# Sixteen-head attention: the causal mask of a diagonal added by one 128-row product per head instead of two 64-row products

## The chip, the cores and the metric

The kernel is one program on one core of a Trainium2 chip. The metric is the time on the device in microseconds, the median of several runs. The core has a matrix engine (PE; its weight loads are shown as PEld), a vector engine (DVE), a scalar engine (ACT), a general engine (POOL) and a queue that issues transfers (SP, shown as SPq).

## The reference

Four transformer layers run on 16 batches of 512 positions, each position a vector of 128. Each layer modulates, normalises, applies an attention, then a feed-forward part. The attentions of layers 0 and 1 are the ones that matter here: 16 heads of 8 dimensions each, causal.

```python
# layer 0; layer 1 is alike, without rope and biases, and its mask adds -1e10
scores = jnp.einsum('bhqd,bhkd->bhqk', Q, K)
causal = jnp.triu(jnp.ones((n, n), dtype=bool), k=1)
scores = jnp.where(causal, -jnp.inf, scores)
attn = jax.nn.softmax(scores / jnp.sqrt(jnp.float32(HEAD_DIM)), axis=-1)
ctx = jnp.einsum('bhqk,bhkd->bhqd', attn, V)
```

Layer 3 also has 16 heads, but no mask. Layer 2 has one wide head. Layer 1's feed-forward part is itself a small transformer with a local attention; it adds its band mask in its own way (lines 2334 to 2342: a product of 128 rows with the identity, then the scores in 64 rows) and is not changed, but its rows are used below.

## The kernel before, in words

`heads16_phase` (line 375) does the 16-head attention of layers 0, 1 and 3. It works through **steps**, one batch apart, and each step has 20 **slots** in a causal layer. The work of three batches overlaps in a step: the maxima of batch i, the probabilities of batch i-1 (or i-2), the projections of batch i+2.

In each slot PE does, in this order: a projection or other full product where the slot has one (`project`, line 614; output product, line 693; V, line 702; transposes of the maxima, line 687); then `a_pair`, the scores of a slot with queries on the partitions, into two PSUM banks of `PA`; then `b_pair`, the scores with keys on the partitions, into two banks of `PB`; then, in 16 of the 20 slots, `pv_pack` (line 674), probabilities times values for four heads, in tiles of 128 rows by 32 columns.

Heads go in pairs. Q and K are split into bf16 terms, so that a head's product has 48 rows (51 in `b_pair`, with the maximum). Head e of a pair lies on partitions 64e and up. So the two products of a pair use the two 64-row halves of the array, and PE runs them side by side. Because of the causal shape a score product is 128, 256, 384 or 512 columns wide, and a slot holds one or two such segments of a head, each with one 128 x 128 diagonal block. `Stream` (line 343) lays the segments out. In every five slots, `a_pair` has 8 diagonals per head (1, 2, 2, 1, 2) and `b_pair` has 8 (1, 1, 2, 2, 2).

On the diagonal block half the scores must be masked. `mask` (inner function, lines 616 to 627) adds -1e30 there by further products into the same bank. It splits the 128 mask rows into two halves of 64 rows: `net.select[rows, 0]` and `net.select[rows, 1]` are the upper and lower 64 rows of the identity, as weights of 64 rows by 128 columns, and `net.select[rows, 2]` or `[rows, 3]` holds the mask's triangle. The half that reaches all columns takes 128 columns per diagonal, the other 64. Each is done for e = 0 and e = 1, on the two halves of the array. All products of `a_pair` and `b_pair` are thus in tiles of 64 rows.

DVE reads `PA` with one maximum-reduction per slot (line 938) over both banks; `PA` has two such pairs of banks, so PE may be two slots ahead. ACT reads `PB` with one exponential per head (line 784), and `PB` has three single banks: `b_pair` of a slot may start once the first exponential of the slot before is done. PE, DVE and ACT each take their work strictly in the order of the code and wait by semaphores (`pa_made`, `pa_used`, `pb_made`, `pb_used`). In slot 14 DVE also waits for a transfer (the sums, line 930), and in four slots (two in layer 1) DVE first takes a projection out of `PA` (line 908 or 910).

`modulation_phase` (line 88) opens the program. SP issues the loads one after another: modulation input and weights, constants, eight small loads for `select` (lines 120 to 123), then `X` in four loads. ACT's first operation (line 131) waits for all loads but `X`, and starts a chain ACT, DVE, PE (line 168), DVE that ends the phase.

Of the kernel before, what the change touches and what calls it, by code (L numbers as in the profile page):

```python
# [7 lines left out]
BF16 = mybir.dt.bfloat16  # L8
# [6 lines left out]
P = 128  # L15
# [51 lines left out]
def load_shared(net, ctx):  # L67
    nc, d = net.nc, net.d

    def sb(name, shape, dt=F32):  # L70
        return ctx.enter_context(nc.sbuf_tensor(name, shape, dt))

    net.passed = nc.alloc_semaphore("passed")
    net.X = sb("X", [P, B, S])
    net.MOD = sb("MOD", [P, 4, 6, B])
    net.ident = sb("ident", [P, P])
    net.center = sb("center", [P, P])
    net.mean = sb("mean", [P, P])
    net.ident_b = sb("ident_b", [P, P], BF16)
    net.H = sb("H", [P, B, S])  # L80
    net.eps = sb("eps", [P, 1])
    net.w3 = sb("w3", [P, B * 3])
    net.chosen = sb("chosen", [1, B * 2], U32)
    net.mask_qk = sb("mask_qk", [P, P], BF16)
    net.select = sb("select", [P, 4, P], BF16)


def modulation_phase(net):

    nc, d = net.nc, net.d  # L90
    with ExitStack() as ctx:
        def sb(name, shape, dt=F32):
            return ctx.enter_context(nc.sbuf_tensor(name, shape, dt))

        cT = sb("cT", [P, 4, B])
        sig = sb("sig", [P, 4, B])
        wm = sb("wm", [P, 4, 6 * P])
        maskf = sb("maskf", [P, 5, P])
        ge = sb("ge", [P, 4, B])
        ab = sb("ab", [P, 4, B])  # L100
        ps = ctx.enter_context(nc.psum_tensor("mod_ps", [P, 4, 6, B], F32))
        loaded = nc.alloc_semaphore("mod_loaded")
        x_loaded = nc.alloc_semaphore("x_loaded")
        ex = nc.alloc_semaphore("mod_exp")
        si = nc.alloc_semaphore("mod_silu")
        mm = nc.alloc_semaphore("mod_products")
        ch = nc.alloc_semaphore("mod_dve_chain")
        block = ctx.enter_context(nc.Block())

        @block.sync  # L110
        def _(sp):
            sp.dma_start(cT[:], d["cT"].rearrange("l p b -> p l b")).then_inc(loaded, 16)
            sp.dma_start(wm[:], d["wmod"].rearrange("l p n -> p l n")).then_inc(loaded, 16)
            sp.dma_start(net.ident[:], d["k_ident"]).then_inc(loaded, 16)
            sp.dma_start(net.center[:], d["k_center"]).then_inc(loaded, 16)
            sp.dma_start(net.mean[:], d["k_mean"]).then_inc(loaded, 16)
            sp.dma_start(maskf[:, 4], d["k_mask"][0]).then_inc(loaded, 16)
            for e in range(2):
                rows = slice(64 * e, 64 * e + 64)
                sp.dma_start(maskf[rows, 0], d["k_ident"][0:64]).then_inc(loaded, 16)  # L120
                sp.dma_start(maskf[rows, 1], d["k_ident"][64:128]).then_inc(loaded, 16)
                sp.dma_start(maskf[rows, 2], d["k_mask"][0, 0:64]).then_inc(loaded, 16)
                sp.dma_start(maskf[rows, 3], d["k_mask"][1, 64:128]).then_inc(loaded, 16)
            for b in range(0, B, 4):
                sp.dma_start(net.X[:, b:b + 4], d["xT"][:, b:b + 4]).then_inc(x_loaded, 16)
            sp.wait_ge(x_loaded, 64)

        @block.scalar
        def _(act):
            act.wait_ge(loaded, 96 + 128)  # L130
            nc.scalar.activation(sig[:], cT[:], ACT.Exp, scale=-1.0).then_inc(ex, 1)

        @block.vector
        def _(dve):
            n = [0]

            def link(ins):
                n[0] += 1
                ins.then_inc(ch, 1)
                dve.wait_ge(ch, n[0])  # L140

            dve.wait_ge(ex, 1)
            link(nc.vector.tensor_scalar(sig[:], sig[:], 1.0, None, ALU.add))
            link(nc.vector.reciprocal(sig[:], sig[:]))
            nc.vector.tensor_tensor(sig[:], sig[:], cT[:], ALU.mult).then_inc(si, 1)
            nc.vector.memset(net.eps[:], 1e-5)
            nc.vector.tensor_copy(net.ident_b[:], net.ident[:])
            nc.vector.tensor_copy(net.mask_qk[:], maskf[:, 4])
            nc.vector.tensor_copy(net.select[:], maskf[:, 0:4])
            dve.wait_ge(mm, 1)  # L150
            M = net.MOD
            link(nc.vector.tensor_copy(M[:], ps[:]))
            for j in (1, 4):
                link(nc.vector.tensor_scalar(M[:, :, j], M[:, :, j], 1.0, None, ALU.add))
            for j in (2, 5):

                link(nc.vector.tensor_scalar(ge[:], M[:, :, j], 0.0, None, ALU.is_ge))
                link(nc.vector.tensor_scalar(ge[:], ge[:], 2.0, -1.0, ALU.mult, ALU.add))
                link(nc.vector.tensor_tensor(ab[:], M[:, :, j], ge[:], ALU.mult))
                link(nc.vector.tensor_scalar(ab[:], ab[:], 0.25, None, ALU.max))  # L160
                link(nc.vector.tensor_tensor(M[:, :, j], ge[:], ab[:], ALU.mult))

        @block.tensor
        def _(pe):
            pe.wait_ge(si, 1)
            for l in range(4):
                for j in range(6):
                    last = nc.tensor.matmul(ps[:, l, j], wm[:, l, j * P:(j + 1) * P], sig[:, l],
                                            start=True, stop=True)
            last.then_inc(mm, 1)  # L170
# [204 lines left out]
def heads16_phase(net, name, layer, causal, rope, w_sum):  # L375

    nc, X, H, d = net.nc, net.X, net.H, net.d
    gate = net.MOD[:, layer, 2]
    scale = float(1.0 / np.sqrt(np.float32(DH8)))
    with ExitStack() as ctx:  # L380
        def sb(n, shape, dt=F32):
            return ctx.enter_context(nc.sbuf_tensor(name + n, shape, dt))
# [19 lines left out]
        st = Stream(causal, rope)  # L402
# [12 lines left out]
        PA = ctx.enter_context(nc.psum_tensor(name + "PA", [P, 4, S], F32))  # L415
        PB = ctx.enter_context(nc.psum_tensor(name + "PB", [P, 3, S], F32))
# [43 lines left out]
        loaded = nc.alloc_semaphore(name + "loaded")  # L460
# [129 lines left out]
        def _(pe):  # L590
# [22 lines left out]
                at_least(pe, pa_used, used_a.before(i, ("Q", n)))  # L613
                nc.tensor.matmul(PA[:, 2 * made_a.slot(par, ("Q", n))], wqk[:, n], H[:, i + 2], start=True, stop=True).then_inc(pa_made, 1)

            def mask(bank, diagonals, pieces):

                k0 = diagonals[0] // P
                by = (diagonals[-1] - diagonals[0]) // P or 1
                done = []  # L620
                for which, of, c0, c1, to in pieces:
                    for e in range(2):
                        rows = slice(64 * e, 64 * e + 64)
                        out = bank(e).rearrange("p (k c) -> p k c", c=P)[:, k0:diagonals[-1] // P + 1:by, to:to + c1 - c0]
                        piece = net.select[rows, of, c0:c1].unsqueeze(1).broadcast_to([64, len(diagonals), c1 - c0])
                        done.append(nc.tensor.matmul(out, net.select[rows, which], piece, start=False, stop=which == pieces[-1][0]))  # L626
                return done[-2:]

            def a_pair(b, i, par, k):
                bank = 2 * made_a.slot(par, ("a", k))  # L630
                at_least(pe, pa_used, used_a.before(i, ("a", k)))
                if k % st.per_group == 0:
                    stacked[k // st.per_group].wait(pe, b, 64)
                done = []
                for n, (pr, t, c) in enumerate(st.a[k]):
                    w = P * (t + 1) if causal else S
                    for e in range(2):
                        rows = slice(64 * e, 64 * e + TERMS)
                        done.append(nc.tensor.matmul(PA[:, bank + e, c:c + w], QS[rows, par, pr, t * P:(t + 1) * P], KS[rows, par, pr, 0:w],  # L639
                                                     start=(n == 0), stop=not causal))  # L640
                if causal:
                    done = mask(lambda e: PA[:, bank + e], [c + P * t for pr, t, c in st.a[k]], [(0, 2, 0, 128, 0), (1, 2, 0, 64, 64)])
                for mm in done[-2:]:
                    mm.then_inc(pa_made, 1)

            def b_pair(b, i, par, k, s):
                bank = [ring_b.slot(0, ("b", s, e)) for e in range(2)]
# [3 lines left out]
                done = []  # L651
                for n, (pr, t, c) in enumerate(st.b[k]):
                    q0 = P * t if causal else 0
                    for e in range(2):
                        rows = slice(64 * e, 64 * e + TERMS + 3)
                        done.append(nc.tensor.matmul(PB[:, bank[e], c:c + S - q0], KS[rows, par, pr, t * P:(t + 1) * P], QS[rows, par, pr, q0:S],  # L656
                                                     start=(n == 0), stop=not causal))
                if causal:
                    done = mask(lambda e: PB[:, bank[e]], [c for pr, t, c in st.b[k]], [(0, 3, 64, 128, 0), (1, 3, 0, 128, 0)])
                for mm in done[-2:]:  # L660
                    mm.then_inc(pb_made, 1)

# [2227 lines left out]
```

## Time and profile before

| what | us |
|---|---|
| median of 3 runs | 6144.11 (6137.29 to 6147.71) |
| the profiled execution | 6168.16 |
| its span, first to last instruction | 6166.0 |
| PE busy, of the span | 5082.9 (82%) |
| DVE busy | 3501.2 (57%) |
| ACT busy | 3147.4 (51%) |
| POOL busy | 2512.3 (41%) |

The mean granted PE clock is 0.899 of full speed. The stages follow each other with little overlap, so a stage's time is read from its own window: layer 0's causal stage has its masks from 100.2 to about 719 us of the span, layer 1's up to 1800.6 us. A PE record's length includes some 0.16 us of latency after its last column, which overlaps the next product; what a product keeps the array for is therefore read from the distance between the starts of two records. A line with "x2" or "x4" on PE joins records that follow each other closely.

### The profile page before, as it was taken

The page shows a single profiled execution, that of the slowest core. Times are in us where ns is not written, and L with a number is a line of the kernel's source. Part 1 is how long each engine was busy: PE and PEld are TensorE (multiplying, and loading weights), DVE is VectorE, ACT ScalarE, POOL GpSimd, SP SyncE. Part 2 cuts the span into 40 slices and gives each one's busy share as a digit, 9 for nine tenths or more (in the row PEclk, how much of TensorE's full clock was granted, in tenths as well). Part 3 has the DMA queues.
Part 4 walks back from the last instruction along what each step waited for, and adds up shares of the span by engine and source line. Part 5 has one row for each costly group of instructions (what it writes and reads, how often), then busy time and mean ns, then how long its engine had stood idle before and what let it go on. Part 6 is the DMA issues. An engine that isn't in the chain of part 4 may idle for free. (4 is left out here: it accounts for less than half of the span.)

```text
span 6166.0 us, 105844 instructions
## 1 busy us (share of the span) xinstructions
PE 5082.9 (82%) x38207; PEld 2620.5 (42%) x38217; DVE 3501.2 (57%) x5633; ACT 3147.4 (51%) x7104; POOL 2512.3 (41%) x2126
## 2 busy tenths in 40 slices
PE   6999779888876999988999998874237999874995
PEld 2444334344433666643566663342112222241784
DVE  5777422487744666643666654565338999730233
ACT  2666633366663666642566663342014888831542
POOL 3333100222206888841788871116562232116025
PEclk7999989899997999998999999986557999976997
DMA  3343111133310000011000000011112333211123
GB/s 99 108 120 110 40 45 48 57 111 103 108 44 20 6 7 8 5 56 45 6 8 6 6 3 4 2 28 41 36 32 65 95 89 96 59 46 49 52 76 90
DMA packets 329515, 312.95 MB, mean 51 GB/s; under 512 B 78758, under 2 KB 279106, under 8 KB 327106
## 3 DMA queue, kind: packets, MB, share of 16 engines
q1 hardware_dynamic: 312642, 285.77, 16.2%
q0 software_dynamic: 16384, 20.69, 1.2%
q8 instruction: 303, 4.96, 0.3%
q14 instruction: 186, 1.52, 0.1%
HBM read 172.15 MB, written 136.32 MB: 50 GB/s over the span
## 5 line engine op out<-in xcount | busy, mean ns | idle before, releaser
L784 ACT ACTIVATE a_prob<-a_PB 128x512 f32<-128x512 f32 x2304 | 1253.4, 598 | 456.9 <-PE a_PB L626 342.7
L674 PE MATMUL a_PO<-a_prob,a_V 128*32 128x256 f32 (+3 forms) x8192 | 715.0, 422 | 22.6 <-ACT a_cn L757 22.3
L938 DVE TENSOR_REDUCE a_blocks<-a_PA 128x8 f32<-128x1024 f32 x512 | 602.0, 1214 | 37.4 <-PE a_PA L626 35.0
L941 DVE TENSOR_REDUCE a_neg<-a_PA 128x2 f32<-128x1024 f32 x512 | 590.8, 1212 | 34.8 <-PE a_PA L639 34.7
L639 PE MATMUL a_PA<-a_KS,a_QS 48*128 48x512 bf16 (+3 forms) x3072 | 469.0, 344 | 112.9 <-DVE a_blocks L938 71.0
L2538 DVE TENSOR_REDUCE f1a_neg<-f1a_PA 128x2 f32<-128x384 f32 (+1 forms) x512 | 266.7, 521 | 488.4 <-PE f1a_PA L2340 487.9
L2468 POOL TENSOR_TENSOR f1a_prob<-f1a_prob,f1a_inv 128x384 f32<-128x384 f32 (+1 forms) x512 | 394.2, 773 | 283.3 <-DVE f1a_inv L2542 283.3
L656 PE MATMUL a_PB<-a_QS,a_KS 51*128 51x512 bf16 (+3 forms) x3072 | 448.3, 329 | 56.6 <-ACT a_prob L784 54.9
L2432 ACT ACTIVATE f1a_pt<-f1a_PT 128x512 f32<-128x512 f32 (+1 forms) x512 | 278.7, 544 | 348.5 <-PE f1a_PT L2349 344.7
L2425 ACT ACTIVATE f1a_prob<-f1a_PA,f1a_neg 128x192 f32<-128x192 f32 (+1 forms) x1024 | 405.3, 404 | 67.9 <-DVE f1a_neg L2538 67.8
L639 PEld LDWEIGHTS a_PA<-a_KS,a_QS 48*128 48x128 bf16 x3072 | 123.5, 94 | 635.5 <-DVE a_blocks L938 199.6
L2477 POOL TENSOR_TENSOR f1a_ss<-f1a_ss,f1a_power 128x16 f32<-128x16 f32 x128 | 372.5, 2910 | 0.9
L838 POOL TENSOR_TENSOR a_qk<-a_qk,a_t 128x512 f32<-128x512 f32 x64 | 81.3, 1270 | 688.2 <-DVE a_t L908 688.2
L2473 POOL TENSOR_TENSOR f1a_qk<-f1a_qk,f1a_rot 128x1024 f32<-128x1024 f32 x128 | 301.0, 2352 | 65.0 <-DVE f1a_rot L2524 65.0
L2349 PE MATMUL f1a_PT<-ident,f1a_prob 128*128 128x128 f32 x1792 | 308.0, 289 | 1.9 <-POOL f1a_prob L2468 1.1
L2360 PE MATMUL f1a_PO<-f1a_pt,f1a_v 128*64 128x128 f32 x3584 | 308.8, 287 | 0.1
L2340 PE MATMUL f1a_PA<-f1a_kT,f1a_qT 64*128 64x192 f32 (+1 forms) x2048 | 293.0, 363 | 0.0
L2030 POOL DMA_INDIRECT f_rows<-tokens_out,f_slot x128 | 132.5, 1035 | 314.0 <-DMA tokens_out<-f_rows 220.2
L674 PEld LDWEIGHTS a_PO<-a_prob,a_V 128*32 128x32 f32 x8192 | 163.3, 108 | 227.6 <-issue 126.8
L2481 POOL TENSOR_TENSOR f1a_qk<-f1a_qk,f1a_ss 128x1024 f32<-128x1024 f32 x128 | 243.5, 1903 | 10.1
L2413 ACT ACTIVATE f1a_sq<-f1a_PJ 128x1024 f32<-128x1024 f32 x128 | 131.2, 1025 | 216.8 <-PE f1a_PJ L2321 216.8
L1180 ACT ACTIVATE f_hid<-f_ph,f_bias 128x512 f32<-128x512 f32 x192 | 131.8, 687 | 199.5 <-PE f_ph L1148 199.0
(416 smaller groups left out, 10391.4 us busy)
## 6 DMA issues: line engine op xcount, KB each, us to landing
a_spill<-a_qkp SPq DMA_DIRECT2D x96, 384.0 KB
a_QS<-a_spill SPq DMA_DIRECT2D x384, 96.0 KB, 2.5
a_KS<-a_spill SPq DMA_DIRECT2D x384, 96.0 KB, 2.5
a_spill<-a_qkp SPq DMA_DIRECT2D x96, 256.0 KB
a_raw<-a_cn SPq DMA_DIRECT2D x192, 72.0 KB
a_spill<-a_qkp SPq DMA_DIRECT2D x96, 128.0 KB
f_rows<-tokens_in SPq DMA_DIRECT2D x78, 128.0 KB
tokens_out<-f_rows SPq DMA_DIRECT2D x78, 128.0 KB
```

Of the source, the lines that this page charges most:

```text
L639: done.append(nc.tensor.matmul(PA[:, bank + e, c:c + w], QS[rows, par, pr, t * P:(t + 1) * P], KS[rows, par, pr, 0:w], start=(n == 0), sto ...
L656: done.append(nc.tensor.matmul(PB[:, bank[e], c:c + S - q0], KS[rows, par, pr, t * P:(t + 1) * P], QS[rows, par, pr, q0:S], start=(n == 0) ...
L674: mm = nc.tensor.matmul(PO[32 * j:32 * j + 32, first:last], V[:, par, t, 8 * e + pr], prob[:, k % st.ring, e, c + first - q0:c + last - q0 ...
L784: nc.scalar.activation(prob[:, k % st.ring, e], PB[:, ring_b.slot(0, ("b", s, e))], ACT.Exp, scale=scale).then_inc(pb_used, 1)
L938: nc.vector.tensor_reduce(to, of, AX, ALU.max).then_inc(pa_used, 1)
L941: nc.vector.tensor_reduce(neg[:, t, pr], PA[:, bank:bank + 2], AX, ALU.max, negate=True).then_inc(pa_used, 1)
L2349: tr = nc.tensor.transpose(PT[:, 2 * e + kt], prob[:, u % 4, e, kt * P:(kt + 1) * P], ident)
L2360: mm = nc.tensor.matmul(PO[e * DH64:(e + 1) * DH64, hp], v[:, par, t - 1 + kt, h * DH64:(h + 1) * DH64], pt[:, u % 2, e, kt], start=(kt == ...
L2425: nc.scalar.activation(prob[:, u % 4, e, c0:], PA[:, u % 2, e, c0:2 * P], ACT.Exp, bias=neg[:, u % 4, e:e + 1], accum_out=total[:, u % 4, ...
L2468: nc.gpsimd.tensor_tensor(pr, pr, inv[:, u % 4].unsqueeze(2).broadcast_to([P, 2, 2 * P - c0]), ALU.mult).then_inc(normed.sem, 1)
L2473: nc.gpsimd.tensor_tensor(qk[:, t], qk[:, t], rot[:], ALU.add).then_inc(joined.sem, 1)
L2477: nc.gpsimd.tensor_tensor(ss[:, t], ss[:, t], power[:], ALU.pow).then_inc(rooted.sem, 1)
```

## The change

`mask` becomes one product per head over all 128 rows: the identity `net.ident_b` (bf16, 128 x 128, already there) as weights, and the whole mask block as the moving operand, 128 columns per diagonal. It is done first for e = 0, then for e = 1. The order of everything else stays. `net.select` goes, a second mask tile `net.mask_kq` comes, and seven of the small loads of the opening go.

```diff
-    net.select = sb("select", [P, 4, P], BF16)
+    net.mask_kq = sb("mask_kq", [P, P], BF16)
...
-            for e in range(2):
-                rows = slice(64 * e, 64 * e + 64)
-                sp.dma_start(maskf[rows, 0], d["k_ident"][0:64]).then_inc(loaded, 16)
-                sp.dma_start(maskf[rows, 1], d["k_ident"][64:128]).then_inc(loaded, 16)
-                sp.dma_start(maskf[rows, 2], d["k_mask"][0, 0:64]).then_inc(loaded, 16)
-                sp.dma_start(maskf[rows, 3], d["k_mask"][1, 64:128]).then_inc(loaded, 16)
+            sp.dma_start(maskf[:, 0], d["k_mask"][1]).then_inc(loaded, 16)
...
-            act.wait_ge(loaded, 96 + 128)
+            act.wait_ge(loaded, 96 + 16)
...
-            nc.vector.tensor_copy(net.select[:], maskf[:, 0:4])
+            nc.vector.tensor_copy(net.mask_kq[:], maskf[:, 0])
...
-            def mask(bank, diagonals, pieces):
+            def mask(bank, diagonals, of):
...
-                done = []
-                for which, of, c0, c1, to in pieces:
-                    for e in range(2):
-                        rows = slice(64 * e, 64 * e + 64)
-                        out = bank(e).rearrange("p (k c) -> p k c", c=P)[:, k0:diagonals[-1] // P + 1:by, to:to + c1 - c0]
-                        piece = net.select[rows, of, c0:c1].unsqueeze(1).broadcast_to([64, len(diagonals), c1 - c0])
-                        done.append(nc.tensor.matmul(out, net.select[rows, which], piece, start=False, stop=which == pieces[-1][0]))
-                return done[-2:]
+                piece = of[:].unsqueeze(1).broadcast_to([P, len(diagonals), P])
+                return [nc.tensor.matmul(bank(e).rearrange("p (k c) -> p k c", c=P)[:, k0:diagonals[-1] // P + 1:by], net.ident_b[:], piece,
+                                         start=False, stop=True) for e in range(2)]
...
-                    done = mask(lambda e: PA[:, bank + e], [c + P * t for pr, t, c in st.a[k]], [(0, 2, 0, 128, 0), (1, 2, 0, 64, 64)])
+                    done = mask(lambda e: PA[:, bank + e], [c + P * t for pr, t, c in st.a[k]], net.mask_qk)
...
-                    done = mask(lambda e: PB[:, bank[e]], [c for pr, t, c in st.b[k]], [(0, 3, 64, 128, 0), (1, 3, 0, 128, 0)])
+                    done = mask(lambda e: PB[:, bank[e]], [c for pr, t, c in st.b[k]], net.mask_kq)
```

## Rows read from the trace of the kernel before

**Rows 1.** Windows: length, busy us of PE, PEld, DVE, ACT, POOL, PEclk, DMA, GB/s

```profile
101.00:168.70 67.70, 53.96 (x508) 23.63 (x508) 55.94 (x66) 19.04 (x34) 21.24 (x23) 0.74 0.22 72
168.70:612.80 444.10, 413.85 (x5254) 186.18 (x5251) 352.00 (x421) 294.37 (x552) 148.71 (x156) 1.00 0.40 113
612.80:678.10 65.30, 57.95 (x824) 27.37 (x820) 50.11 (x54) 46.39 (x88) 3.81 (x4) 1.00 0.27 67
678.10:722.50 44.40, 34.41 (x412) 12.32 (x408) 5.01 (x14) 33.98 (x65) 3.54 (x4) 0.96 0.10 22
...
1272.70:1698.40 425.70, 382.89 (x5188) 177.28 (x5187) 333.76 (x396) 294.04 (x552) 106.09 (x120) 0.98 0.38 107
1698.40:1763.10 64.70, 57.36 (x812) 26.94 (x814) 50.49 (x53) 46.25 (x87) 3.10 (x3) 0.97 0.27 69
```

**Rows 2.** Groups, 168.7 to 612.8 us: busy us, mean ns | idle before

```profile
L784 ACT ACTIVATE a_prob<-a_PB 128x512 f32<-128x512 f32 x480 | 261.3, 599 | 143.8 <-PE a_PB L626 142.1 <-PE a_PO L674 1.7
L938 DVE TENSOR_REDUCE a_blocks<-a_PA 128x8 f32<-128x1024 f32 x193 | 227.3, 1213 | 8.1 <-PE a_PA L626 8.0
...
L639 PE MATMUL a_PA<-a_KS,a_QS 48*128 48x512 bf16 (+3 forms) x768 | 93.9, 302 | 17.7 <-DVE a_blocks L938 15.6 <-DVE a_halves L938 0.6
L656 PE MATMUL a_PB<-a_QS,a_KS 51*128 51x512 bf16 (+3 forms) x768 | 92.4, 298 | 12.2 <-ACT a_prob L784 11.3
...
L938 DVE TENSOR_REDUCE a_halves<-a_PA 128x8 f32<-128x1024 f32 x48 | 58.5, 1218 | 11.4 <-PE a_PA L626 11.4
```

**Rows 3.** Groups, 1272.7 to 1698.4 us, PE's longest wait

```profile
L639 PE MATMUL a_PA<-a_KS,a_QS 48*128 48x512 bf16 (+3 forms) x768 | 94.7, 305 | 30.9 <-DVE a_blocks L938 30.8
```

**Rows 4.** Line 626: ns min/median/max, first to last start us, shapes

```profile
L626 PE MATMUL a_PA<-select x2560: 187/218/418, 100.6 to 1762.8; 64*128 64x128 bf16 x98, 64*128 64x256 bf16 x60, 64*128 64x64 bf16 x39
```

**Rows 5.** PE timeline, one slot of layer 0: start us, length us

```profile
402.71 0.39 PE L639 MATMUL a_PA<-a_KS,a_QS 48*128 48x512 bf16 x2
402.94 0.25 PE L626 MATMUL a_PA<-select 64*128 64x128 bf16 x4
403.03 0.38 PE L656 MATMUL a_PB<-a_QS,a_KS 51*128 51x512 bf16 x2
403.25 0.25 PE L626 MATMUL a_PB<-select 64*128 64x64 bf16 x4
403.43 0.42 PE L674 MATMUL a_PO<-a_prob,a_V 128*32 128x128 f32 x8
403.78 1.12 PE L614 MATMUL a_PA<-H,a_wqk 128*128 128x512 f32 x2
404.84 0.34 PE L639 MATMUL a_PA<-a_KS,a_QS 48*128 48x384 bf16 x2
```

**Rows 6.** PE timeline, local attention of layer 1

```profile
2502.68 1.02 PE L2321 MATMUL f1a_PJ<-f1a_w,f1a_hs 128*128 128x512 f32 x2
2503.54 0.33 PE L2337 MATMUL f1a_PA<-f1a_band,ident_b 128*128 128x192 bf16 x2
2503.80 0.59 PE L2340 MATMUL f1a_PA<-f1a_kT,f1a_qT 64*128 64x192 f32 x4
2504.32 0.66 PE L2349 MATMUL f1a_PT<-ident,f1a_prob 128*128 128x128 f32 x4
2504.91 0.33 PE L2360 MATMUL f1a_PO<-f1a_pt,f1a_v 128*64 128x128 f32 x2
```

**Rows 7.** Timeline and one transfer (us to landing) of the opening

```profile
3.34 0.44 SPq L117 DMA_DIRECT2D maskf<-in_k_mask  x1
3.82 0.56 SPq L120 DMA_DIRECT2D maskf<-in_k_ident  x1
...
8.90 2.26 SPq L125 DMA_DIRECT2D X<-in_xT  x4
11.20 0.26 ACT L131 ACTIVATE sig<-cT 128x64 f32<-128x64 f32 x1 [9.19 <-DMA maskf<-in_k_mask]
...
wm<-in_wmod SPq DMA_DIRECT2D x1, 1536.0 KB, 6.6
```

## The prediction

> **What bounds the kernel now.** I first cut the two causal stages into windows. From 168.7 to 612.8 us layer 0 does 12 full steps: 241 of the 20-slot steps' maximum reductions lie in it [rows 2], so a step takes 444.1 / 12 = 37.0 us. Layer 1's 12 full steps take 425.7 / 12 = 35.5 us [rows 1]. In layer 0 PE is busy 413.85 of 444.1 us, DVE 352, ACT 294; in layer 1 PE 383 of 426, DVE 334, ACT 294. PE's clock is 1.00 and 0.98, so nearly always at 2.4 GHz. Next I looked at who waits. ACT's exponentials sat idle 143.8 us, nearly all for the mask products of `b_pair`; DVE's reductions 19.5 us for those of `a_pair`; PE's score products only 17.7 + 12.2 us, for DVE and ACT [rows 2], and 30.9 us for DVE in layer 1 [rows 3]. So PE sets the pace, with some waits left, more of them in layer 1.
>
> Last, the timeline, since busy time hides what a product holds the array for. From the score product to the mask are 0.23 us for 512 columns (213 ns at 2.4 GHz), from there to the next scores 0.09 us for 128 + 64 columns (80 ns): both heads of a pair together, nothing lost between scores and masks. From the masks of `b_pair` to the pack at line 674 are 0.18 us for 80 ns of columns [rows 5]. The difference, **0.10 us, appears wherever the shape of the tiles changes** (64x128, 128x32, full 128x128). The local attention shows it in the order that the change makes: line 2321 to 2337, both full 128x128, 0.86 us for 0.85 us of columns (f32 takes four passes, 2048 columns in 0.85); line 2337 to 2340, full to 64 rows, 0.26 us for 2 x 192 columns = 0.16: 0.10 lost; line 2340 to 2349, 64 rows to full, 0.52 us for 0.32: 0.10 lost, and another 0.10 because the first f32 weights after a change are loaded in the open [rows 6]. For bf16 that second part is about 0.01: 0.23 us after a change against 0.22 without one, for the same 512 columns [rows 5]. A change of tile shape with bf16 behind it therefore costs 0.105 us.
>
> **The changes, part by part.**
>
> *The columns.* A 64-row mask pair takes 128 + 64 columns per diagonal with both heads at once; the 128-row products take 128 per diagonal and head, one after the other: 64 more per diagonal. With 16 diagonals per five slots, 64 in a step: 4096 columns, **+1.7 us a step**.
>
> *The tile changes.* Before, a slot is 64-row from the first score to the last mask. After, scores, mask, scores, mask alternate: three more changes in each of 20 slots, and one more after the last mask in the 4 slots without a pack, where the next scores follow directly. From mask to pack there was a change already. 64 changes x 0.105 = **+6.7 us a step**.
>
> *Fewer instructions.* 80 products and their loads fewer a step. Concurrent tiles start 3 to 7 ns apart in line with the slot of [rows 5], about 4 ns for each of 5254 / 12 = 438 records [rows 1]: -0.3 us a step. Loading the same identity twice hides behind the product before it, as the two of line 2337 do (2 x 192 columns and one change fill their 0.26 us [rows 6]).
>
> *Sum for PE.* Layer 0 before: 66048 columns-passes a step (scores 20480, masks 12288, packs 20480, projections 8192, output, V and transposes 4608) = 27.5 us; 39 changes x 0.105 = 4.1; 438 starts x 4 ns = 1.7: own work 33.3 us, so 3.7 of the 37.0 are waits. Layer 1 (59904 columns, 36 changes): 30.5 us, 5.0 of waits. After: 33.3 + 8.1 = **41.4** and **38.6 us**. That is beyond DVE's 352 / 12 = 29 us and ACT's 25 to 28, so most waits vanish: where PE waited for a reduction or an exponential, it now arrives later. What stays? Each step has one wait of DVE for the sums, and projection slots are uneven. I leave 0.6 us a step in layer 0 and 0.9 in layer 1, between none and all of today's 3.7 and 5.0; nearer to none, since PE now leads DVE by 12 and 10 us a step. Steps of 42.0 and 39.5 us: 12 x 5.0 + 12 x 4.0 = **+108 us**.
>
> *The ends of the stages.* The next window, 65.3 and 64.7 us for 39 slots, has no projections but all masks [rows 1]: own work after is 41.4 less the 3.4 us and 4 changes of four projections, 37.5 us a step (layer 1, two projections: 36.7), with 0.6 and 0.9 of waits 39/20 of it is 74 and 73: +17 together. In the first two steps (67.7 us, DVE busy 56 [rows 1]) PE has room: I take +1.5 each, bounds 0 and +10. In the tail (44.4 us, ACT busy 34 [rows 1]) only `b_pair` is left, 20 slots and a few: PE gains 4.6 us of work, much beside ACT; I take +2.5 each, bounds 0 and 4.6. Together **+25**.
>
> *The opening.* Seven loads fewer, 0.64 us of SP each: the `X` loads start at 4.4 instead of 8.90 us. ACT's first operation waited 9.19 us until 11.20 for the last small load. But `wm`, 1.5 MB, issued at 1.23, lands 6.6 us later at 7.8 [rows 7], with four 64 KB constants and the new one behind it. I take 9.7: **-1.5 us**, bounds 0 and -3.4. `X` lands early enough. DVE's copy for `select` lies beside PE's modulation products and costs nothing.
>
> *Not shown by the trace:* a change from 64 rows to full with bf16 on both sides. The nearest rows bound it: 0.08 us (the raw 0.10 less rounding of two starts) below, and above 0.165 us, the whole latency of a product (218 ns for 128 columns of 53 [rows 4]), should it be waited out. I take 0.105, as both neighbours give it. Below it 64 x 0.025 = 1.6 us a step less, above it 3.8 more.
>
> The Trainium skill, TensorE: Matmul & The Clock Gate, section Single matmul latency, has the drain of one product at some 175 ns whatever the clock. Taken as the price of each change that would be 11.2 us a step in place of 6.7; the trace has 0.10 at every change in both layers, so the sum goes by that. The Trainium skill, TensorEngine Tiling, Instruction Overhead, gives each product a floor of some 60 cycles, so that halving the products would save 80 x 25 ns = 2 us a step. Here the 64-column piece does not stand above its columns: 0.09 us hold 192 of them.
>
> Against the profiled 6168.2 us: +108 +25 -1.5 = **+132**. The median lies 24 us below that execution: 6144.1 + 132 = **6276 us**.
>
> **Rivals.**
> 1. *The waits stay* (15%). The time to a finished pair grows too: scores, change, mask e = 0, mask e = 1. If DVE and ACT were released late by as much, today's waits would stay on top. Then all of PE's new work counts: per stage some 1010 changes x 0.105 + 27.3 us of columns - 1.3 = 132; two stages 264, less 1.5: 6406 us. For it: ACT idles 143.8 us for exactly these masks. Against: PE may run two slots ahead of DVE.
> 2. *A change costs the full latency*, 0.165 us (9%). Steps of 45.8 and 43.3 us, 12 x (8.8 + 7.8) = 199, ends +40: 6382 us. Against: six places with 0.10.
> 3. *The changes are hidden* (6%, the other side). If from scores to a mask and back PE loses nothing because the identity stands ready in its second set of weights and products of the same bank follow on, only the 1.7 us of columns stay, and 3.7 and 5.0 us of waits take them in; the opening gains 1.5: 6142.6 us. It decides below (3.7 - 1.7) / 64 = 31 ns a change. Against: line 2337 to 2340 writes one bank and still loses 0.10.
> 4. *The diff does not do what it says*: the products for e = 0 and e = 1 could still run side by side. They can't: both fill all 128 rows. I give it nothing.
>
> **How the numbers follow.** Forecast 70%, on its own from 6220 (no waits left: 12 x (4.4 + 3.1) + ends 15 - 1.5 = +104, and -28 for 28 steps with 64 changes of 0.09 us) to 6350 (2 to 3 us of today's waits stay in each step). To leave out no more than 2 in 10 the range goes on to 6382, the second rival: 6222 to 6385. 0.2% of this kernel, 12 us, is about what a measurement can tell. Faster 0.02 and same 0.04 share the third rival, slower 0.94.
>
> **What would show it.** In the profile after: 2560 mask products at the new line, 128*128; 0.10 us lost on either side of each mask in the timeline; steps of 42.0 and 39.5 us in windows from reduction to reduction; ACT idle for PE well above 143.8 us; PE's idle before lines 639 and 656 under 15 us; ACT's first operation near 9.7 us. I am wrong if the steps come out below 39 us (changes hidden), or above 44 (latency paid or waits kept); if the clock of these windows falls from 1.00 the columns are dearer, which none of these sums has in it.

## The result: 2.1% slower, and where the time went

The changed kernel takes 6274.63 us (median of 4 runs, 6270.95 to 6283.94), against 6144.74 before (4 runs): **ratio 1.0211, interval 1.0198 to 1.0223, +130 us**. Forecast were 6276 us and +132. On a second chip, where the kernel before takes 5972.55 us, it takes 6100.76: ratio 1.0213 (1.0198 to 1.0229), +128 us.

The profiled execution after has a span of 6268.8 us, before 6166.0. Cut at the start of each stage, these +102.8 us are: opening -1.8, causal stage of layer 0 +67.2 (713.4 to 780.6), causal stage of layer 1 +55.4 (669.7 to 725.1), together +120.8; and -18 in stages that no edit touches, 13 of it in the last feed-forward stage (691.2 to 677.8). The profiled execution before lay 24 us over its median, and in the run with the new opening alone (below), where that stage is the same too, it took 675.7: so this is scatter between executions and not the change. So the change costs about 121 us by the traces and 130 by the medians. How far one trace can be trusted shows in that same run: its causal stages differ from the kernel before in nothing, and took 703.4 and 675.6 us in place of 713.4 and 669.7, with steps of 36.8 and 35.6 us in place of 37.0 and 35.5. A difference between two traces of under 10 us in a stage, or under 0.3 us in a step, says little.

The windows of the stages, cut from reduction to reduction as in [rows 1], after (same columns):

```profile
97.20:166.20 69.00, 59.99 (x390) 19.16 (x390) 56.54 (x67) 19.04 (x34) 21.29 (x23) 0.79 0.23 76
166.20:668.80 502.60, 502.60 (x4298) 167.82 (x4294) 356.10 (x420) 298.12 (x553) 149.26 (x156) 1.00 0.35 99
668.80:742.50 73.70, 72.65 (x672) 24.54 (x670) 51.34 (x53) 47.18 (x88) 5.10 (x5) 1.00 0.23 59
742.50:788.00 45.50, 37.13 (x357) 11.15 (x356) 5.05 (x13) 33.97 (x65) 2.27 (x2) 1.00 0.10 21
1338.70:1805.80 467.10, 465.54 (x4228) 157.36 (x4224) 340.58 (x396) 298.08 (x553) 106.80 (x120) 1.00 0.35 99
1805.80:1877.60 71.80, 70.38 (x668) 23.99 (x666) 51.76 (x54) 47.27 (x88) 3.10 (x3) 1.00 0.22 53
```

In the 12 full steps of layer 0 PE is now busy 502.60 of 502.60 us: no gap is left that is longer than the latency in its records. A step takes 41.9 us (502.6 / 12) in place of 37.0; in layer 1 38.9 in place of 35.5. DVE's busy time is 1 to 2% above that before, and spreads over the longer time. The groups of layer 0's window, after, to be laid beside [rows 2]:

```profile
L774 ACT ACTIVATE a_prob<-a_PB 128x512 f32<-128x512 f32 x481 | 261.1, 594 | 197.0 <-PE a_PB L616 197.0
L928 DVE TENSOR_REDUCE a_blocks<-a_PA 128x8 f32<-128x1024 f32 x192 | 231.5, 1219 | 36.4 <-PE a_PA L616 34.6
...
L646 PE MATMUL a_PB<-a_QS,a_KS 51*128 51x128 bf16 (+3 forms) x772 | 94.3, 302 | 0.0
L629 PE MATMUL a_PA<-a_KS,a_QS 48*128 48x512 bf16 (+3 forms) x768 | 93.9, 302 | 0.0
L616 PE MATMUL a_PB<-mask_kq,ident_b 128*128 128x256 bf16 (+1 forms) x480 | 83.8, 256 | 0.0
L616 PE MATMUL a_PA<-mask_qk,ident_b 128*128 128x256 bf16 (+1 forms) x480 | 83.8, 256 | 0.0
L928 DVE TENSOR_REDUCE a_halves<-a_PA 128x8 f32<-128x1024 f32 x48 | 58.7, 1222 | 28.3 <-PE a_PA L616 28.1
```

PE's score products had idled 17.7 and 12.2 us for DVE and ACT [rows 2]; now 0.0 and 0.0 (in layer 1, line 629 idles 1.6). What moved is the waiting: ACT idles 197.0 us for the masks in place of 142.1, DVE's reductions 62.7 in place of 19.4. The mask products are 480 on each side instead of 960, each 256 ns long in the mean instead of 227, as their pieces are wider.

Where PE's new time lies shows in its timeline, after, in one slot of layer 0:

```profile
502.69 0.39 PE L629 MATMUL a_PA<-a_KS,a_QS 48*128 48x256 bf16 x4
503.02 0.39 PE L616 MATMUL a_PA<-mask_qk,ident_b 128*128 128x256 bf16 x2
503.34 0.39 PE L646 MATMUL a_PB<-a_QS,a_KS 51*128 51x512 bf16 x2
503.67 0.28 PE L616 MATMUL a_PB<-mask_kq,ident_b 128*128 128x128 bf16 x2
503.88 0.85 PE L664 MATMUL a_PO<-a_prob,a_V 128*32 128x384 f32 x8
504.66 1.12 PE L683 MATMUL a_PA<-a_heads,a_wo 128*128 128x512 f32 x2
505.72 0.39 PE L629 MATMUL a_PA<-a_KS,a_QS 48*128 48x512 bf16 x2
```

From the scores at 502.69 (2 x 256 columns, 213 ns) to the masks at 503.02 are 0.33 us; from the masks (two products of 256 columns, 213 ns) to the next scores at 503.34, 0.32; from these scores (512 columns) to their masks, 0.33. Each is 0.11 to 0.12 above its columns. Before, the first and the third of these distances were 0.23 and 0.22 with the same columns, and the one between masks and scores 0.09 [rows 5]. From masks to pack (256 columns, 107 ns) are 0.21: the change that was there before and stays.

### The profile page after: what moved, and what is told of

It reads as the page before. It is cut to its first block and busy times, and to the rows that moved or that the text cites. A ratio compares the mean times of both kernels' runs of the same rounds, so it can differ in the third digit from the quotient of the medians.

```text
span 6268.8 us, 100727 instructions
## 1 busy us (share of the span) xinstructions
PE 5298.4 (85%) x35657; PEld 2564.4 (41%) x35657; DVE 3517.5 (56%) x5633; ACT 3158.4 (50%) x7104; POOL 2515.4 (40%) x2126
## 3 DMA queue, kind: packets, MB, share of 16 engines
q0 software_dynamic: 16384, 20.69, 1.2%
## 5 line engine op out<-in xcount | busy, mean ns | idle before, releaser
L928 DVE TENSOR_REDUCE a_blocks<-a_PA 128x8 f32<-128x1024 f32 x512 | 616.6, 1218 | 113.7 <-PE a_PA L616 107.5
L1170 ACT ACTIVATE f_hid<-f_ph,f_bias 128x512 f32<-128x512 f32 x192 | 131.8, 687 | 197.5 <-PE f_ph L1138 197.0
```

The lines of the kernel that those rows point to most:

```text
L928: nc.vector.tensor_reduce(to, of, AX, ALU.max).then_inc(pa_used, 1)
```

## The experiments

The first question was whether the time comes from the changes of tile shape or from the columns (and heads no longer side by side). Two runs change one of them, starting from the kernel before.

**Columns only.** Both 64-row pieces of the mask are made 128 columns wide. `net.select` gets two more blocks (4 and 5) for this, with four more small loads in the opening, which the cut below leaves out.

```diff
-                    done = mask(lambda e: PA[:, bank + e], [c + P * t for pr, t, c in st.a[k]], [(0, 2, 0, 128, 0), (1, 2, 0, 64, 64)])
+                    done = mask(lambda e: PA[:, bank + e], [c + P * t for pr, t, c in st.a[k]], [(0, 2, 0, 128, 0), (1, 4, 0, 128, 0)])
...
-                    done = mask(lambda e: PB[:, bank[e]], [c for pr, t, c in st.b[k]], [(0, 3, 64, 128, 0), (1, 3, 0, 128, 0)])
+                    done = mask(lambda e: PB[:, bank[e]], [c for pr, t, c in st.b[k]], [(0, 5, 0, 128, 0), (1, 3, 0, 128, 0)])
```

> The kernel before with both 64-row pieces of the mask 128 columns wide: the 4096 columns a step that the change adds, with no change of tile shape, and 4 more small loads in the opening (about +2.5 us). Theory: PE's own work grows by 1.7 us a step, to 35.0 and 32.2 us, and today's waits of 3.7 and 5.0 us take in about half: +0.9 us a step, total near 6172 us (6147 to 6200). Rival (the columns are what costs): +100 us or more, near 6250 us.

Measured: ratio 1.0030 (1.0019 to 1.0042), +19 us. Steps of 37.5 and 35.8 us: of 1.7 us more work a step only 0.5 and 0.3 arrive, less than the half that I had set. (All experiments but the last four were timed on two chips on both of which the kernel before takes 5972 us; ratios and differences are against that. The kernel before was profiled on a slower chip only, and steps are compared with that trace; that this is allowed shows below, in the changed kernel's second run.) Its window of layer 0:

```profile
166.50:616.80 450.30, 431.17 (x5254) 192.31 (x5254) 350.75 (x420) 294.26 (x552) 148.57 (x156) 1.00 0.40 111
```

PE is busy 19 us of the window less than its length; in [rows 1] it was 30. Added columns fill gaps first.

**Changes of shape only.** The 64-row masks stay. A product of 128 rows with one zero column is set between scores and mask of each pair.

```diff
                 if causal:
+                    nc.tensor.matmul(PA[:, bank, 0:1], net.ident_b[:], net.mask_qk[:, 0:1], start=False, stop=False)
...
                 if causal:
+                    nc.tensor.matmul(PB[:, bank[0], 0:1], net.ident_b[:], net.mask_qk[:, 0:1], start=False, stop=False)
```

> The kernel before, with one product of 128 rows and a single zero column between the scores and the mask of each a_pair and b_pair: 80 changes of tile shape a step more and hardly any column. Theory: own work 33.3 + 80 x 0.105 + 40 x 0.025 = 42.7 us a step in layer 0 and 39.9 us in layer 1, waits under 0.5 us: steps of 43 and 40 us, total near 6300 us. Rival (changes of shape are hidden, the time comes from columns and lost concurrency): 40 products of one column are 1 us a step, total near 6160 us.

Measured: ratio 1.0308 (1.0291 to 1.0326), +183 us; steps of 43.1 and 40.1 us, as worked out. The total is 27 us above my sum: the two stages are 178 us longer than in the trace before, 129 of it in the 24 full steps and 49 at their ends, where I had counted too little. The timeline of PE in this run:

```profile
502.12 0.38 PE L657 MATMUL a_PB<-a_QS,a_KS 51*128 51x384 bf16 x4
502.43 0.18 PE L660 MATMUL a_PB<-mask_qk,ident_b 128*128 128x1 bf16 x1
502.54 0.34 PE L626 MATMUL a_PB<-select 64*128 64x128 bf16 x4
...
503.38 0.39 PE L639 MATMUL a_PA<-a_KS,a_QS 48*128 48x512 bf16 x2
503.70 0.18 PE L642 MATMUL a_PA<-mask_qk,ident_b 128*128 128x1 bf16 x1
503.81 0.26 PE L626 MATMUL a_PA<-select 64*128 64x128 bf16 x4
503.91 0.33 PE L657 MATMUL a_PB<-a_QS,a_KS 51*128 51x384 bf16 x2
```

From the scores at 503.38 (512 columns) to the one-column product are 0.32 us, 0.11 above the columns; from it to the mask in 64 rows another 0.11, with one column in it. So 80 changes with no columns to speak of cost more than the whole change under study. The rival, that took columns and lost concurrency for the cause, had +15 us here.

**Half of them.** The one-column product in `b_pair` alone.

```diff
                 if causal:
+                    nc.tensor.matmul(PB[:, bank[0], 0:1], net.ident_b[:], net.mask_qk[:, 0:1], start=False, stop=False)
```

> The kernel before with the one-column product of 128 rows in b_pair alone: 40 changes of tile shape a step more, half of the run with both. Theory (PE's own work, and waits that give way): own work 33.3 + 4.2 + 0.5 = 38.0 us in layer 0, 35.2 in layer 1, and 1.5 to 2 us of waits: steps of 39.7 and 37.1 us, +75 us. Rival (each change adds its full price whatever the waits): half of what the run with both added, +91 us.

Measured: ratio 1.0147 (1.0132 to 1.0163), +87 us; steps of 40.0 and 37.3 us, against 39.7 and 37.1 by the theory. The total is nearer to the rival's +91 than to my +75, and layer 0 sides with the rival too: the first 40 changes add 3.0 us a step there and the second 40 add 3.1, so the waits did not take in the first of them and pass on the later ones. Only layer 1 goes as the theory said: 1.8 us for the first 40, 2.8 for the second.

**The changed kernel with fewer changes of shape.** The order in a slot becomes scores, scores, masks, masks: `a_pair` and `b_pair` end before their masks and hand back a function that issues them.

```diff
-                    if has(i):
-                        a_pair(i, i, par, s)
+                    last = []
+                    if has(i):
+                        last.append(a_pair(i, i, par, s))
...
+                    for finish in last:
+                        finish()
```

> The changed kernel with the order inside a slot turned to scores of a, scores of b, mask of a, mask of b: the same products and columns, but 40 changes of tile shape fewer a step (63 instead of 103 in layer 0). Theory (the changes of shape cost): PE's own work falls by 40 x 0.107 = 4.3 us a step, from 41.97 to 37.7 us in layer 0 and from 38.8 to 34.5 us in layer 1; some waits come back (about 1.5 us a step, since a mask of a now also stands behind the wait of b's scores for ACT): steps of 39.2 and 36.3 us, total near 6200 us. Rival (128-row products are dear because the two heads no longer run side by side, and by their number): nothing changes, 6275 us.

Measured: ratio 1.0138 (1.0121 to 1.0155), +81 us: **a third of the loss is won back** with the same products and columns, against +128 for the changed kernel on a chip of the same speed. Steps of 39.9 and 37.0 us, 0.7 above what I expected of each. Its timeline, and two of its waits (us in total, times, longest) in the 12 steps of layer 0:

```profile
502.38 0.39 PE L629 MATMUL a_PA<-a_KS,a_QS 48*128 48x384 bf16 x4
502.61 0.38 PE L649 MATMUL a_PB<-a_QS,a_KS 51*128 51x384 bf16 x4
502.93 0.39 PE L616 MATMUL a_PA<-mask_qk,ident_b 128*128 128x256 bf16 x2
503.15 0.38 PE L616 MATMUL a_PB<-mask_kq,ident_b 128*128 128x256 bf16 x2
503.47 0.64 PE L670 MATMUL a_PO<-a_prob,a_V 128*32 128x256 f32 x8
```

```profile
ACT a_prob L785 <- PE a_PB L616: 174.7, 204, 2.0
...
PEld a_PB L649 <- ACT a_prob L785: 33.0, 68, 0.6
```

Only 502.61 to 502.93 (512 columns) and 503.15 to 503.47 hold a change now; 502.38 to 502.61 and 502.93 to 503.15 are bare columns. The 0.7 us more than expected probably sit in the second view: weight loads for the scores of `b_pair` wait 33.0 us for ACT, in place of 20.7 before the change and 13.2 in the changed kernel, and a mask of `a_pair` now stands behind this wait. No run separates this from other waits.

**A product inside one shape.** The changed kernel with each mask product issued twice.

```diff
-                                         start=False, stop=True) for e in range(2)]
+                                         start=False, stop=again == 1) for again in range(2) for e in range(2)]
```

> The changed kernel with each mask product issued twice (it adds -2e30): 16384 columns and 80 products a step more, no change of tile shape more. Theory: PE is the bound without slack, so the step grows by the columns, 6.8 us, and 80 x 3 ns: steps of 49.0 and 45.9 us, total near 6490 us. Rival (a 128-row product costs its full latency, 0.165 us beyond its columns, wherever it stands): 13 us a step on top of the columns, about 6900 us.

Measured: ratio 1.0564 (1.0546 to 1.0582), +333 us against +345 expected by difference; steps of 48.7 and 45.6 us, +6.8 and +6.7. 16384 columns take 6.8 us: that is the columns and nothing else. With PE busy from end to end, its work enters the time in full:

```profile
170.60:754.60 584.00, 584.00 (x5255) 245.64 (x5256) 359.75 (x421) 298.27 (x553) 149.24 (x156) 1.00 0.30 85
```

Behind another of its shape, a 128-row product costs its columns; what costs extra is the way into and out of its shape.

**Is it PE that sets the pace before?** The kernel before, without mask products.

```diff
-                if causal:
+                if False:
                     done = mask(lambda e: PA[:, bank + e], [c + P * t for pr, t, c in st.a[k]], [(0, 2, 0, 128, 0), (1, 2, 0, 64, 64)])
```

and the same in `b_pair`; the last score product of a bank then closes it.

> The kernel before without any mask product (the mask is left out of layers 0 and 1): PE's own work falls by 12288 columns and 160 products, to 27.6 us a step in layer 0 and 24.7 us in layer 1. Theory: DVE (29 us a step with 12 us of other causes to wait) and ACT now set the pace, so that only part is won: steps of 34 and 33 us, total 70 us below before. Rival (PE alone sets the pace even before): steps of 31.9 and 30.4 us, 150 us below.

Measured: ratio 0.9970 (0.9961 to 0.9979), only -17 us, where I expected -70 and the rival -150. 5.8 us less work of PE a step shorten it by 0.7 us in layer 0 (36.3) and 1.2 in layer 1 (34.3). In its window PE is busy 374.50 of 435.40 us, and its clock is no longer full, 0.95 in place of 1.00:

```profile
164.70:600.10 435.40, 374.50 (x3338) 113.88 (x3334) 348.05 (x420) 294.12 (x553) 148.73 (x156) 0.95 0.41 114
```

```profile
L640 PE MATMUL a_PA<-a_KS,a_QS 48*128 48x512 bf16 (+3 forms) x768 | 98.3, 316 | 43.8 <-DVE a_blocks L940 38.4 <-DVE a_t L910 4.5 <-DVE a_halves L940 0.9
L658 PE MATMUL a_PB<-a_QS,a_KS 51*128 51x512 bf16 (+3 forms) x768 | 97.4, 312 | 16.1 <-ACT a_prob L786 14.7
```

PE's scores wait 43.8 and 16.1 us. One rival has to be looked at: that PE does set the pace and the lower clock ate the gain. A mean of 0.95 is about a tenth of the time at 1.2 GHz instead of 2.4, so the clock can hide at most some 0.05 x 36.3 = 1.8 us a step (an estimate). With it the gain would be 2.5 us in layer 0 and under 3 in layer 1, not 5.8. So PE alone does not set the pace. What else does is read from the waits and not tested: DVE's wait for the transfer of the sums, in the 12 steps of layer 0, is 35.1 us here, 25.1 before and 12.6 in the changed kernel. It grows as PE's work shrinks.

Read together, the runs give roughly one curve. PE's own work is a model, worked out as in the prediction at full clock and with 0.105 us a change; the steps are measured; the last column is their difference:

| kernel | own work, us a step, layer 0 / 1 | step, us | left as waits |
|---|---|---|---|
| no masks | 27.5 / 24.7 | 36.3 / 34.3 | 8.8 / 9.6 |
| before | 33.3 / 30.5 | 37.0 / 35.5 | 3.7 / 5.0 |
| columns only | 35.0 / 32.2 | 37.5 / 35.8 | 2.5 / 3.6 |
| masks last | 37.1 / 34.3 | 39.9 / 37.0 | 2.8 / 2.7 |
| changes in `b_pair` | 38.0 / 35.2 | 40.0 / 37.3 | 2.0 / 2.1 |
| changed kernel | 41.4 / 38.6 | 41.9 / 38.9 | 0.5 / 0.3 |
| changes only | 42.7 / 39.9 | 43.1 / 40.1 | 0.4 / 0.2 |
| masks twice | 48.5 / 45.7 | 48.7 / 45.6 | 0.2 / 0 |

Below some 33 us of PE work a step hardly notices; from 33 to 41 it pays about half in the mean; above 41 it pays nearly all. The curve is not exact: with the masks last there is less work than with the changes in `b_pair`, yet more waiting, so the order in a slot counts too. The change crosses this bend: of its 8.1 us in each step 3.2 to 4.7 were taken in.

**The changed kernel again**, on the second chip.

> The changed kernel once more, beside the runs of this chip, on which the kernel before takes 5972 us in place of 6145. Theory: the difference lies in the two causal stages, which are bound by PE and DVE and not by memory, so it is the same +130 us (6101 us) with steps of 41.9 and 38.9 us. Rival (the difference scales with whatever makes this chip faster): less than 100 us.

Measured: +128 us and steps of 41.9 and 38.9 us, the same to 0.01 us. What makes that chip 173 us faster lies outside these stages: 142 us in the last feed-forward stage (677.8 to 536.2) and 31 in that of layer 2 (428.2 to 397.1).

**Fewer changes of shape in the kernel before.** Two packs in one slot:

```diff
-                self.packs += [(g, 0, at + 1, at + 4, 2), (g, 1, at + 3, at + 5, 2), (g, 3, at + 3, at + 6, 2), (g, 2, at + 4, at + 7, 2)]
+                self.packs += [(g, 0, at + 1, at + 5, 2), (g, 1, at + 3, at + 5, 2), (g, 3, at + 3, at + 7, 2), (g, 2, at + 4, at + 7, 2)]
```

> The kernel before with the packs of probabilities times values done two in one slot, in 8 slots of a step instead of 16: 16 changes of tile shape fewer, nothing else in number. Theory: own work falls by 1.7 us a step, but the slots become uneven (1.9 us of packs in one, none in the next, where b_pair then waits for ACT), so that between 1 us is won and 1 us lost a step: total -30 to +30 us, middle -5. Rival (changes of shape count in full everywhere): -45 us.

Measured: ratio 1.0076 (1.0063 to 1.0090), +45 us, outside what I had allowed; steps of 38.1 and 35.9 us. 1.7 us less work of PE, and the step is 1.1 us longer in layer 0, 0.4 in layer 1. Its timeline shows why:

```profile
500.72 1.71 PE L674 MATMUL a_PO<-a_prob,a_V 128*32 128x512 f32 x16
...
502.37 0.39 PE L639 MATMUL a_PA<-a_KS,a_QS 48*128 48x512 bf16 x2
...
502.99 0.38 PE L639 MATMUL a_PA<-a_KS,a_QS 48*128 48x384 bf16 x4
...
503.24 1.09 ACT L784 ACTIVATE a_prob<-a_PB 128x512 f32<-128x512 f32 x2 [1.27 <-PE a_PB L626]
503.89 0.12 PEld L656 LDWEIGHTS a_PB<-a_QS,a_KS 51*128 51x128 bf16 x4 [0.58 <-ACT a_prob L784]
503.89 0.39 PE L656 MATMUL a_PB<-a_QS,a_KS 51*128 51x384 bf16 x4 [0.36 <-ACT a_prob L784]
...
504.38 0.38 PEld L674 LDWEIGHTS a_PO<-a_prob,a_V 128*32 128x32 f32 x16 [0.16 <-ACT a_prob L784]
504.38 0.86 PE L674 MATMUL a_PO<-a_prob,a_V 128*32 128x128 f32 x16
```

PE spends 1.65 us on two packs (500.72 to 502.37), and ACT, which has three banks ahead of it, runs dry and idles 1.27 us before 503.24; two slots later PE waits 0.36 us for ACT at 503.89. So here uneven slots cost more than 16 changes of shape saved. Two of each four packs also come a slot later, which this run doesn't separate from the unevenness.

**A version that beats both.** Moving the projections, too, makes slots more or less even; that gave the last four runs. They start from the kernel before, with the eight small loads on a semaphore of their own, so that ACT's first operation does not wait for them.

```diff
-            act.wait_ge(loaded, 96 + 128)
+            act.wait_ge(loaded, 96)
...
+            dve.wait_ge(halves_loaded, 128)
             nc.vector.tensor_copy(net.select[:], maskf[:, 0:4])
```

> The kernel before with the eight small loads on a semaphore of their own: ACT's first operation no longer waits for them, DVE's copy of them does; the X loads still stand behind them. Theory: the wait ends with the last of the six first loads, near 9 us of the span in place of 11.2, and the modulation phase ends 2 us earlier, as far as the transfers let it; -2 us, which only the profile can show. Rival (the phase ends with the X loads): no change in the start of layer 0's stage.

Measured: ratio 0.9994 (0.9983 to 1.0005). ACT's first operation starts at 9.39 us in place of 11.20 [rows 7], and layer 0's stage at 25.6 in place of 27.4. It is 1.8 us, too small for the runs to show.

```diff
-        q = [7, 8, 9, 10] if causal else [13, 15, 17, 19]
+        q = [0, 5, 10, 15] if causal else [13, 15, 17, 19]
```

> As the run with the new opening, and the projections at slots 0, 5, 10 and 15 (0 and 10 in layer 1), the slots without a pack, in place of 7 to 10: the same work and changes of shape. Theory (before the change the pace is set jointly: uneven slots make DVE wait 3 us a step for projections): PE's slots become even, a step loses 1 to 2 us, total 25 to 50 us below before. Rival (PE's own work sets the pace): no change. Second rival: the projection at slot 15 comes too late for the split on POOL and the spill, and the step grows.

Measured: ratio 1.0013 (1.0000 to 1.0027). Layer 1's steps became 34.3 us, but layer 0's 38.2: a gain and a loss. The 25 to 50 us that I expected didn't come; the total is near the first rival's "no change", but not for its reason, as the steps did change.

```diff
-        q = [7, 8, 9, 10] if causal else [13, 15, 17, 19]
-        self.q = q if rope else q[::2]
+        q = [0, 5, 7, 10] if causal else [13, 15, 17, 19]
+        self.q = q if rope else [5, 10] if causal else q[::2]
```

> As the run before it with projections at slots 0, 5, 7 and 10 (5 and 10 in layer 1), so that the last is no later than before. Theory: half of the evening out, -10 to -30 us, and no danger of a late spill. Rival: no change.

Measured: ratio 0.9992 (0.9981 to 1.0004). That can't be told from no change, where I expected -10 to -30 us. Steps of 37.4 us in layer 0, 33.7 in layer 1, in place of 37.0 and 35.5. So it helps in layer 1 and not in layer 0. The traces point at the projection in slot 0. In layer 0 PE's score products now wait 20.4 us (run before) and 17.5 us (this run) in the 12 steps until DVE has taken out a projection of Q or K, always behind the one of slot 0; in the run with the new opening alone the list of waits has no such row. Layer 1 of the run before, which has one in slot 0 too, waits 14.2 us; layer 1 of this run, with slots 5 and 10, doesn't. Layer 0 without a projection in slot 0 was not run.

```diff
         q = [7, 8, 9, 10] if causal else [13, 15, 17, 19]
-        self.q = q if rope else q[::2]
+        self.q = q if rope else [5, 10] if causal else q[::2]
```

> The kernel before with the new opening and the projections moved in layer 1 alone, to slots 5 and 10; layer 0 keeps slots 7 to 10, since moving them there made its steps longer (37.4 and 38.2 us in place of 37.0). Theory: layer 1's steps are 33.7 us as in the run before this one, its stage 14 us shorter, the opening 2 us: -16 us, a ratio near 0.9975. Rival: what layer 1 gains is within what its steps scatter by, ratio 1.000.

Measured: **ratio 0.9972 (0.9960 to 0.9984), 6130.85 against 6147.01 us**: as expected, and faster than both kernels, if by only 0.3%. Layer 1's stage takes 653.3 us in place of 669.7, its steps 33.7 in place of 35.5. Waits in layer 1's window (who waits <- for whom: us, times, longest), first of the run with the new opening alone, then of this one; PE waits 13.9 us for DVE in place of 31.3, DVE 13.4 for projections in place of 19.0, and 24.4 for the transfer of the sums in place of 38.8, which is the largest drop of the three:

```profile
DVE a_comp L932 <- DMA a_comp<-a_raw: 38.8, 12, 4.2
PE a_PA L641 <- DVE a_blocks L940: 31.3, 32, 3.2
...
DVE a_qk L912 <- PE a_PA L616: 19.0, 24, 1.5
```

```profile
DVE a_comp L932 <- DMA a_comp<-a_raw: 24.4, 12, 2.9
...
PE a_PA L641 <- DVE a_blocks L940: 13.9, 14, 1.9
DVE a_qk L912 <- PE a_PA L616: 13.4, 24, 0.9
```

## Why the prediction was right, point by point

*The price of a change of shape*, 0.105 us, was read from other pairs of shapes and held for the new one: 0.11 to 0.12 from scores to mask and back, 0.10 from mask to pack. Neither bound (0.08, 0.165) was reached. The second rival (full latency, 6382 us) is out: its steps were 45.8 and 43.3 us. The third, hidden changes, is out by the run with one-column products, which has changes and hardly any columns.

*Columns*, 1.7 us a step: as PE work shown by the run with doubled masks (6.7 to 6.8 us for 16384 columns, so 1.7 for 4096).

*The sum for PE and the waits left.* Forecast 41.4 + 0.6 and 38.6 + 0.9, measured 41.9 and 38.9: +58.5 and +41.4 us over the 12 steps of each layer, where I had 60 and 48. The first rival (waits stay, 6406 us) is out: PE's idle time before lines 629 and 646 went to 0.0 in layer 0 and 1.6 in layer 1. I had said under 15 us. That layer 0 comes out within 0.1 us is partly luck, for two terms cancel. The waits of 0.6 us that I left did not stay. But a full f32 product after a change costs more than 0.105 us: from 504.66 to 505.72 in the timeline above are 1.06 us, for 0.85 us of columns and one change, so 0.10 is over. All 48 projections of layer 0's window take this long. The prediction had seen this second part in [rows 6] and left it out of its sum. With four projections, the output product and V it is some 0.6 us a step in layer 0, with two projections and V some 0.3 in layer 1 (estimates from these distances), which is about all that stands above 41.4 and 38.6. So PE hardly waits any more, and of the waits in the table about 0.6 and 0.3 us are such work in every row. In layer 1, where I had left 0.9, the waits made my sum too large.

The prediction found no overhead on small products since the 64-column piece does not stand above its columns. That excludes a time added to each product, but not a floor that is lower than 64 columns; no run here tests one.

*The ends*: +8.7 and +14.0 us, 22.7 together, forecast 25. *The opening*: -1.8, forecast -1.5; ACT's first operation starts at 9.44 us, forecast 9.7:

```profile
3.85 0.51 SPq L118 DMA_DIRECT2D maskf<-in_k_mask  x1
4.41 2.10 SPq L120 DMA_DIRECT2D X<-in_xT  x4
9.44 0.26 ACT L126 ACTIVATE sig<-cT 128x64 f32<-128x64 f32 x1 [7.43 <-DMA maskf<-in_k_mask]
```

The terms sum to 121 us against the 132 forecast; the medians say 130. That the medians come nearer to the forecast than the terms do is partly luck: the stages scatter by some 10 us from trace to trace, and against the trace with the new opening alone the two causal stages would have grown by 127 us.

*What was not right* is the first reading: "So PE sets the pace, with some waits left." The run without masks shows that PE does not set it alone: taking 5.8 us of work off PE gains about 1. I had read 93% busy and DVE's and ACT's waits for PE as proof. The sum did not rest on it, since it went by PE's own work after, which is beyond the bend. A forecast for a change that takes work off PE would have failed on it, and mine for that run did, by 53 us of 70. The one for the packs in pairs failed too: I had named the unevenness, but put its price at 0.7 to 2.7 us a step, where it was 2.8 in layer 0 (1.1 lost and 1.7 not won) and 2.1 in layer 1, and had nothing for the ends of the stages.

## What to carry to other kernels

Count the places where consecutive products of PE change the shape of their tiles, and price each from the distance between starts in the trace of this very kernel; products of few columns are cheap inside one shape and dear between two. Work out PE's own time a step (columns, changes, starts) and compare it with the step: the difference is room that takes in part of new work, and a warning that removing work will gain less than its own time. If the engines share the pace, try how the work is spread over the slots and look at every stage by itself: the same idea won up to 1.8 us a step in layer 1 and lost up to 1.1 in layer 0.

## What the runs showed of the hardware

- A product of one column between two changes holds PE 0.11 us up to the start of the next shape, and the change into it costs 0.11 too: so the price of a change was the same after one column as after 512.
- A full f32 product of 128 x 512 behind a change of shape holds PE 1.06 us for 0.85 us of columns: 0.10 us for the change and 0.10 more, 48 times of 48 in the changed kernel's window of layer 0.
- With the masks left out, PE's granted clock in the window fell from 1.00 to 0.95, though it is still busy 86% of the time. How much more the step would have gained at full clock stays open, but for the bound of 1.8 us above.
- Two of the chips differ by 174 us of 6275 for the changed kernel, and by 0.01 us in the steps of the causal stages.
